# The convolution stage of layer 0 in 64x64 tiles of TensorE, with its quantization redistributed over DVE, POOL and ACT

## The reference, cut to what matters

```
def act_quant(x):
    scale = 127.0 / jnp.clip(jnp.max(jnp.abs(x), axis=-1, keepdims=True), 1e-05)
    return jnp.clip(jnp.round(x * scale), -128, 127) / scale
def weight_quant(w):
    scale = 1.0 / jnp.clip(jnp.mean(jnp.abs(w)), 1e-05)
    return jnp.clip(jnp.round(w * scale), -1, 1) / scale
...
h = bit_linear(x, w1)                                # both operands quantized
h = depthwise_conv1d(h.transpose(0, 2, 1), conv_w, conv_b)   # 3 taps per hidden channel, along the rows
h = jax.nn.silu(h.transpose(0, 2, 1))
return bit_linear(h, w2)
...
x = x + _L0_xattn_ref(...)
x = x + _L0_ffn_ref(_layernorm(x, axis=-1), L0_ffn_w1, L0_ffn_conv_w, L0_ffn_conv_b, L0_ffn_w2)
x = x + _L1_xattn_ref(_layernorm(x, axis=-1), ctx_1024, ...)
```

## Time and profile before

| | |
|---|---|
| time, 3 runs | 1159.99, 1159.32, 1154.71 us; median 1159.32 |
| span of the profiled execution | 1158.0 us (first to last instruction); no time of its own is given for it beside the span, which is 1.3 us under the median |
| busy in that span | PE 1103.8 us (95%), DVE 772.5 (67%), POOL 522.9 (45%), ACT 430.0 (37%) |
| the stage of the change | from 140 to 284 us of the span |

### The profile page before, as it was taken

One profiled execution on the slowest core, in us unless ns is written; L12 is line 12 of the kernel. 1 busy time (PEld: TensorE's weight loads), 2 busy tenths in 40 slices (PEclk: granted clock), 3 DMA queues, 4 the chain that ended last, 5 costly groups with the idle time before them and its releaser, 6 DMA issues.

```text
span 1158.0 us, 21241 instructions
## 1 busy us (share of the span) xinstructions
PE 1103.8 (95%) x7601; PEld 919.3 (79%) x7601; DVE 772.5 (67%) x1711; ACT 430.0 (37%) x890; POOL 522.9 (45%) x505
## 2 busy tenths in 40 slices
PE   9999999999899999999989999999999999999997
PEld 5788888886778856898877999999998687875564
DVE  5899889997887645989962222222222899977784
ACT  2555533234555412121111222222222456654466
POOL 5655224356877121768866111100254757531343
PEclk9999999999999999999988999999999999999999
DMA  6999700000100020000135422311120200000001
GB/s 223 393 397 387 286 1 1 13 12 10 79 1 1 1 103 1 1 2 24 38 137 197 176 109 109 110 36 36 55 88 30 78 10 10 1 1 1 1 28 46
DMA packets 44182, 93.61 MB, mean 81 GB/s; under 512 B 3885, under 2 KB 17998, under 8 KB 41414
## 3 DMA queue, kind: packets, MB, share of 16 engines
q1 hardware_dynamic: 35702, 62.24, 14.9%
q0 software_dynamic: 7104, 29.14, 6.9%
q10 hardware_dynamic: 1296, 1.18, 0.3%
HBM read 39.02 MB, written 51.51 MB: 78 GB/s over the span
## 4 chain that ended last, share of the span: by engine, by line
PE 61%; DVE 21%; POOL 6%; issue 5%; ACT 4%; DMA 2%; POOLq 1%; PEldq 0%; another core or an unknown queue 0%; SPq 0%; DVEq 0%; PEld 0%; ACTq 0%
PE PS L2416 10%; PE PS L2426 10%; PE PS L1109 6%; PE PS L1925 4%; PE PS L2281 3%; PE PS L1122 3%; PE PS L1087 2%; PE PS L1077 2%; DVE scr L1468 2%; PE PS L2270 2%; PE PS L1642 2%; DVE scr L1494 2%; PE PS L1804 2%; POOL big L695 1%; PE PS L1035 1%
## 5 line engine op out<-in xcount | busy, mean ns | idle before, releaser
L2450 ACT ACTIVATE scr<-PS,W 128x128 f32<-128x128 f32 x148 | 53.6, 367 | 191.1 <-PE PS L2416 190.0
L2416 PEld LDWEIGHTS PS<-scr 128*128 128x128 f32 x992 | 116.4, 192 | 5.2 <-issue 2.0
L2416 PE MATMUL PS<-scr 128*128 128x128 f32 x992 | 118.6, 276 | 1.6 <-issue 1.6
L2426 PE MATMUL PS<-scr 128*128 128x256 f32 x496 | 112.2, 379 | 0.0
L2481 DVE TENSOR_SCALAR scr<-PS,W 128x128 f32<-128x128 f32 x148 | 51.2, 350 | 85.2 <-PE PS L2416 85.2
L727 POOL TENSOR_TENSOR scr<-scr,small 128x1232 f32<-128x1232 f32 x32 | 72.0, 2251 | 73.1 <-DVE small L478 72.8
L2426 PEld LDWEIGHTS PS<-scr 128*128 128x128 f32 x496 | 91.8, 190 | 11.2
L2487 DVE TENSOR_TENSOR scr<-PS,W 128x256 f32<-128x256 f32 x37 | 15.7, 425 | 127.1 <-PE PS L2426 122.3
L868 ACT ACTIVATE big<-PS 128x512 f32<-128x512 f32 x144 | 73.1, 523 | 69.1 <-PE PS L1087 67.7
L2527 POOL DMA_DIRECT2D expert_out<-scr x28 | 15.3, 547 | 160.5 <-DVE scr L2487 156.5
L1109 PEld LDWEIGHTS PS<-scr,big 128*128 128x128 f32 x640 | 81.0, 191 | 8.1 <-issue 5.1
(11 more groups left out here) (418 smaller groups left out, 2496.4 us busy)
## 6 DMA issues: line engine op xcount, KB each, us to landing
expert_in<-zeros SPq DMA_DIRECT2D x1, 19712.0 KB, 60.5
expert_out<-zeros SPq DMA_DIRECT2D x1, 19712.0 KB, 113.2
scr<-ew_in POOLq DMA_DIRECT2D x12, 1024.0 KB, 6.6
scr<-expert_in SPq DMA_DIRECT2D x38, 128.0 KB
big<-ew_in POOLq DMA_DIRECT2D x4, 1024.0 KB, 8.9
expert_out<-scr POOLq DMA_DIRECT2D x28, 128.0 KB, 2.0
W<-pack SPq DMA_DIRECT2D x1, 2458.0 KB, 8.7
W<-pack SPq DMA_DIRECT2D x1, 2152.0 KB, 9.0
```

The lines of the kernel that those rows point to most:

```text
L2416: ins = pe.matmul(bank(1 + f % 4, G), e_w1[slot][:, k, f * P:(f + 1) * P], e_xT[:, k, :], start=(k == 0), stop=(k == C - 1))
L2426: ins = pe.matmul(bank(5 + t, D), e_h[:, f, t * P:(t + 1) * P], e_w2[slot][:, f, :], start=(f == 0), stop=(f == FC - 1))
L2450: a.activation(e_h[:, f, :], bank(1 + f % 4, G), ACT.Relu, bias=moe_bias(e, f)).then_inc(s["h_act"], 1)
```

## The change

- The convolution's diagonal matrices are cut into 64x64 blocks. Per pair and tap, four matmuls (row half r of the partitions, chunk c of the pair) take 64 partitions each and write 64 partitions of bank r. The two halves of a PSUM bank then hold the two chunks of the pair, so w2 and the bias are loaded in that permuted order (`hidden_rows_sp`: four DMAs for one; `hidden_biases`: four small ACT copies). The banks are chosen by `conv_bank`.
- The normalization (`rows`) goes from DVE to ACT. The magnitudes are taken by ACT (`absolutes`), and DVE takes maxima of them with plain tensor_tensor instructions in place of a strided reduce.
- The product with the row of scales goes from POOL to DVE (`scaled`). The rounding of the first half (1024 elements per partition) goes from DVE to POOL, that of the second half to ACT in two passes (add, subtract).
- Two copies of scales to full tiles are gone; PE's transposes read the broadcast scales.
- `second_made` and `second_added` come one sample later, and the order on PE and DVE is new.

```
-                for f in (2 * p, 2 * p + 1):
-                    for j in range(3):
-                        ins = pe.matmul(bank(2 + p % 2, S, (f % 2) * S), f_taps[:, f, j, :], f_G[:, f, j:j + S],
-                                        start=(j == 0), stop=(j == 2))
+                for j in range(3):
+                    for r in range(2):
+                        rows = slice(r * HALF, (r + 1) * HALF)
+                        for c in range(2):
+                            f = 2 * p + c
+                            ins = pe.matmul(PS[c * HALF:(c + 1) * HALF, conv_bank(i, p, r), 0:S],
+                                            f_taps[rows, f, j, rows], f_G[rows, f, j:j + S],
+                                            start=(j == 0), stop=(j == 2))
...
-                ch.inc(v.tensor_reduce(f_top[:, n, :], f_y[i % 2][:, n * PAIRS:(n + 1) * PAIRS, :].rearrange("p f s -> p s f"),
-                                       AX.X, ALU.max, apply_absolute_value=True))
+                v.wait_ge(s["abs_ready"], 2 * i + n + 1)
+                v.tensor_tensor(f_top[:, n, :, :], f_abs[n][:, 0:2, :], f_abs[n][:, 2:4, :], ALU.max).then_inc(s["abs_used"], 1)
...
+                ch.link(v.tensor_tensor(f_top[:, 0, :, :], f_top[:, 0, :, :], f_top[:, 1, :, :], ALU.max))
+                v.tensor_tensor(f_amax, f_top[:, 0, 0, :], f_top[:, 0, 1, :], ALU.max).then_inc(s["amax_ready"], 1)
...
+            def scaled(i, n):
+                v.wait_ge(s["row2_ready"], i + 1)
+                y = f_y[i % 2][:, n * PAIRS:(n + 1) * PAIRS, :]
+                v.tensor_tensor(y, y, f_row2.unsqueeze(1).broadcast_to([P, PAIRS, S]),
+                                ALU.mult).then_inc(s["scaled1_ready" if n else "scaled0_ready"], 1)
...
+            def rounded(i, n):
+                if i:
+                    g.wait_ge(s["o_psum"], i)
+                fs = slice(n * PAIRS, (n + 1) * PAIRS)
+                g.wait_ge(s["scaled1_ready" if n else "scaled0_ready"], i + 1)
+                g.tensor_scalar(f_aq[:, fs, :], f_y[i % 2][:, fs, :], ROUND, ROUND, ALU.add,
+                                ALU.subtract).then_inc(s["aq1_ready" if n else "aq0_ready"], 1)
...
             for i in range(B):
-                if i:
-                    scaled(i - 1)
                 if i + 2 < B:
                     ternary_rstd(g, i + 2)
+                if i:
+                    rounded(i - 1, 0)
...
+            def rows(i):
+                a.wait_ge(rstd_ready, i + 1)
+                a.wait_ge(z_ready, T * i)
+                for t in range(T):
+                    ins = a.activation(f_z[:, t, :], X[:, T * i + t, :], ACT.Identity,
+                                       bias=f_shift[i % 2][:, t:t + 1], scale=f_rstd[i % 2][:, t:t + 1])
+                ins.then_inc(s["rows_ready"], 1)
...
+                a.activation(f_abs[n], f_y[i % 2][:, n * PAIRS:(n + 1) * PAIRS, :], ACT.Abs).then_inc(s["abs_ready"], 1)
...
+                a.activation(y, y, ACT.Identity, bias=f_round[:, 0:1]).then_inc(s["lifted"], 1)
+                if i:
+                    a.wait_ge(s["o_psum"], i)
+                a.wait_ge(s["lifted"], i + 1)
+                a.activation(f_aq[:, fs, :], y, ACT.Identity, bias=f_round[:, 1:2]).then_inc(s["aq1_ready"], 1)
```

More of the change, by code:

```diff
@@ L1267, in program @@
         f_rstd = [cut(T) for _ in range(2)]
+        f_shift = [csmall(T) for _ in range(2)]
         cut = Cut(scr)
@@ L1270, in program @@
         f_aq = cut(FC * S, dt=BF16).rearrange("p (f s) -> p f s", f=FC)
-        f_wide2 = cut(T * P).rearrange("p (t n) -> p t n", t=T)
         f_row2 = cut(S)
-        f_top = cut(2 * S).rearrange("p (f s) -> p f s", f=2)
+        f_top = cut(4 * S).rearrange("p (n f s) -> p n f s", n=2, f=2)
         f_amax = cut(S)
+        f_abs = [t.rearrange("p (f s) -> p f s", f=PAIRS) for t in (cut(PAIRS * S), big[:, 3 * C * S * 2:3 * C * S * 2 + PAIRS * S])]
+        assert cut.at <= 12288 - VB_WORDS and 3 * C * S * 2 + PAIRS * S <= C * FF + FC * D
         f_am = csmall(T)
         f_sc = csmall(T)
+        f_am2 = csmall(T)
+        f_sc2 = csmall(T)
         f_deq = csmall(T)
-        f_deq2 = csmall(T)
+        f_deq2 = [csmall(T) for _ in range(3)]
+        f_bias = csmall(FC)
         f_tot = csmall(2 * C)
@@ L1480, in scales @@
[L1480 to L1495 removed]
+                ch.link(v.tensor_reduce(f_am2, bank(AMAX_BANK, T * P).rearrange("p (t n) -> p t n", t=T), AX.X, ALU.max))
@@ L1511, in ffn0_dve @@
             hidden(0, (2, 3))
+            row_scales(1)
+            quant_rounded(v, ch)
             for i in range(B):
-                if i:
-                    scales(i - 1)
-                if i + 1 < B:
-                    quantized(i + 1)
                 if i + 2 < B:
@@ L1540, in ffn0_dve @@
                     sample_rows(v, 1, 0)
-            scales(B - 1)
+            second_added(v, B - 2)
             head_normed(v, 0)
```

239 lines of the change are left out of this document (137 added, 102 removed).

## The result

The changed kernel takes 1141.11 us (median of 4 runs, 1138.22 to 1145.35) against 1159.29 of the kernel before; the ratio is 0.9856, 95% interval 0.9830 to 0.9881. Forecast were 1140 us, 1128 to 1152. The total was right; it is made of three terms, and all three were off, in directions that cancel.

A forecast was written before the change was run, and what follows sets the result against it. PE and DVE were taken to bound the stage together. Gains of 4.7 us at the start, 13.2 in the middle and 1.6 at the end took the span from 1158.0 to 1138.5; with 1.3 for the median, 1140 us (1128 to 1152).

The forecast's parts named there:

- What bounds the kernel: In the stage PE and DVE bind together, 16.50 and 15.98 us busy per sample; only shortening both helps.
- PE's sample, 12.4 us: PE's work per mid-stage sample: 6.14 us of rest, 5.18 of convolution in four parallel tiles, 1.1 for three tile groups.
- slower rival: PE's convolution: column tiles do not run side by side; PE's sample 17.6 us, total about 1165 us; chance 0.12.
- DVE's sample, 12.5 us of its own and 0.3 for POOL's small instructions: DVE per mid-stage sample: 16.5 less 8.5 removed plus 4.5 added; 0.3 for small POOL instructions getting between the products.
- 1.4 us of waiting for POOL's rounding: Per mid-stage sample, one DVE instruction waits for POOL's whole rounding, 1.4 us (bounds 0.9 and 2.34); sample 14.2 us.
- the rule: DVE instructions with two SBUF inputs and POOL instructions reading SBUF exclude each other for a whole instruction; sample 14.2 us.
- the middle: Six samples between statistics landmarks: 98.4 us before, 6 x 14.2 = 85.2 after, a gain of 13.2 us.
- rival without a lock: Mid-stage: POOL's rounding costs DVE no wait; DVE and PE at 12.5 us per sample, total 1128 us; chance 0.15.
- The start, 4.7 us: Stage start through the first sample: the next sample's statistics end 4.7 us earlier (bounds 0 and 6).
- The end, 1.6 us gained: From the last statistics to the last rounding: 16.0 us in place of 17.6, some 2 us of waiting for POOL staying.
- The sum: Start, middle and end of the stage together: 4.7 + 13.2 + 1.6 = 19.5 us gained, giving 1140 us.
- rival of a chain through ACT: ACT's new instructions delay SiLU, convolution and row of scales: sample 15.5 to 16.3 us, total 1149 to 1155; chance 0.15.

The follow-up runs named there:

- reduce_max: Changed kernel with each half's maximum made again by one strided reduce over four features on DVE, and one later maximum less; 1151.44 us.
- full_tiles: Changed kernel with the convolution back in 128x128 matmuls without tiles, weights and biases unpermuted; 1169.76 us, ratio 1.0083 to the kernel before.
- pool_quarter: Changed kernel in which POOL rounds 256 of its 1024 elements and the other 768 are zero (output not the reference's); 1136.16 us, one run.
- round0_dve: Changed kernel with the first half's rounding on DVE ahead of the maxima, none on POOL; 1138.99 us.
- rstd_first: Changed kernel with POOL's 1/std of sample 1 (first norm of layer 1) ahead of its rounding in the last round; 1138.67 us.
- joined: Changed kernel with 1/std ahead of POOL's last rounding, second_made(6) ahead of PE's last maxima, and ACT's bias copies in the first sign pass; 1134.31 us.

## Why the prediction was right, and where it was not

*What bounds the kernel.* Right. From the changed kernel, lengthening either engine alone lengthens the sample: 1.8 us more on DVE give 14.34 us (reduce_max), 3.9 us more on PE (16.65 busy for 12.74) give 17.07 (full_tiles).

*PE's sample, 12.4 us.* Right: 12.74 busy. Against full_tiles (17.07 less 0.42 idle, less the 5.18 that the tiles take off) that is 1.3 us for three groups, where I had 1.1 from one burst of row tiles. The slower rival falls on the group of 48 in 2.75 us. PE has 0.6 us to spare and not 1.8, because the sample became shorter than forecast.

*DVE's sample, 12.5 us of its own and 0.3 for POOL's small instructions.* The 12.5 was right: pool_quarter, where the maxima of a steady sample wait for nothing, has 12.81, of which DVE idles 0.25. The 0.3 was right in size and wrong in kind. The pair of products takes 2.33 us, the 2.3 forecast, with POOL's small instructions beside it; the 0.25 is a wait for PE's `hidden` (L1448). The steady samples of the changed kernel have 13.35 and 13.42. (The instructions with two inputs in SBUF are six per sample, not five: two products, three maxima of 512 elements and one of 256. The sum had all six.)

*1.4 us of waiting for POOL's rounding.* This step failed, in two ways that oppose each other, and the nearness of the total is luck here. I took the length of POOL's instruction for the length of DVE's wait. The length was wrong (3.64 us, outside 0.9 to 2.34), and so was the rule: DVE is held for 0.91 us from POOL's start whether POOL takes 3.64 or 2.78. What DVE then pays is 0.91 less the time by which its first maximum starts later: 0.23, 0, 0.53, 0.82, 0.88 and 0 us in the six rounds of the middle. Against pool_quarter three of the six samples lose nothing by it. In the middle it is 1.7 us in all (79.11 - 77.42), where I had 6 x 1.4 = 8.4. These 6.7 us are a little more than the 6.0 by which the middle was better than forecast (19.2 against 13.2). At 13.2 us a sample the middle lies nearer to my rival without a lock (12.5, chance 0.15) than to the forecast (14.2). Had the rule held with the true length, a sample would have been about 12.8 + 3.6 = 16.4 us, as long as before. The Trainium skill, page SBUF — State Buffer, section SBUF: two separate sides, says that whichever of the two starts first has the shared pair of ports for the whole instruction and the other fully blocks. For this instruction the traces disagree (0.91 of 3.64 us). For the memset beside round0_dve's rounding they nearly agree, since DVE's wait lasts to 202.07 + 1.52 - 0.69 = 202.90 and the memset to 203.05.

*The start, 4.7 us.* Measured 3.1 between landmarks, and 2.2 in absolute time, since this execution came 0.9 us late to the stage (clock 0.88 from 120 to 134 us against 1.00 before). Five other kernels with the same start have 3.6. By those the walk through the first sample was 1.1 us too hopeful; ACT's bias copies are 0.2 of it, the rest I have not taken apart.

*The end, 1.6 us gained.* This step failed: 3.3 us were lost. I had POOL's rounding and the 1/std behind it in the right place but at 1.4 us in place of 3.64, and left out that the rounding first waits for `second_made(5)`. I did not look at PE there at all. Its 5.33 idle us come after the filler of 8, which the change leaves as it was; before, `second_made(6)` stood ahead of that filler and no gap came behind it. The new order puts it behind the maxima, which is in the change and which I did not cost. The runs price the parts, each to about 0.5: 1.8 for the half clock, 0.8 for POOL's order, 1.5 for PE's (the last two overlap with the first, since they too change how long the clock is low). With all but the clock repaired the end is 17.6, with the clock too 16.5, near the forecast 16.0, which had 2 us of waiting for POOL in it.

*The sum.* 2.2 + 19.2 - 3.3 = 18.2 us at the last rounding (19.5 forecast), 18.8 in the span; 1140 against 1141.11. The miss of 6 us in the middle and those of 2.5 and 4.9 at the ends cancelled. The start stayed within its bounds (0 to 6), the middle did not (19.2 gained, where samples of 13.7 to 15.1 us give 7.8 to 16.2), and the end, which had no bounds, came out with the wrong sign. That the total fell on 1140 was luck to that extent.

*ACT.* Its load is 10.34 of 13.35 us (11.2 forecast) and DVE never waited for it in the middle: all of DVE's idle time there is ended by PE. PE waited for it once, 0.96 us at 162.26. The rival of a chain through ACT falls for the middle; at the end it is the next wait once POOL's is gone.

## What to carry to other kernels

Where two engines are level, cost both for every edit, and price the first and the last round by walking every engine's queue there, PE's with its filler too: a steady sample was worth 3.1 us here, and the unsteady end took back as much as one of them. When work moves to an engine for which the trace has no row of that kind, separate how long it takes from how long it holds others up. And a total that fits is no proof of its terms: compare landmark by landmark.

## What the runs showed of the hardware

- Column tiles run side by side as row tiles do: with 64x64 tiles a step of four matmuls of 256 columns takes 0.229 us against 0.216 for one over the full array. Three groups of tiles per sample cost 1.3 us beside their columns.
- POOL's tensor_scalar from f32 to bf16 takes 3.64 us for 1024 elements and 1.07 for 256 with two operations, 2.78 with one; DVE has 0.69 for the same 1024. A DVE instruction with two inputs in SBUF waits for the first 0.91 us of it and then runs at full speed beside it. 0.91 is near what a memset needs for as many elements (1120 ns for 1224; by that rate, an estimate, 0.94 for 1024), and for 256 elements the one instance gives 0.24. That it is the reading of the input is not shown: elements read and written changed together, and a memset, which reads nothing, held DVE's rounding too. Two inputs in SBUF are not needed for a wait: that rounding and L423 in rstd_first (1.45 us for 0.73) have one large input each.
- Contention also stretches POOL: beside DVE's products its instructions of 2 elements take 1.08 and 1.18 us (L205, L198), 0.19 where DVE is otherwise busy (L198 at 247.89). The second of them ends at 188.39, the pair of products at 188.34, so in this direction the hold seems to last for the whole instruction.
- After 5.33, 3.96, 3.42 and 2.04 us without work, PE ran 16 matmuls in 3.52, 3.62, 3.60 and 3.07 to 3.30 us in place of 1.91. With 22 filler matmuls more ahead of them they took 1.91 in the changed kernel, with 9 more 1.92 in joined.
